# Moving ten label loads within one DMA queue: four to later places, six spread out

## What is computed

```python
e = stack([tbl_f[ids[:, f]] for f in range(50)], axis=1)      # 1024 x 50 x 300
q1 = attn_pool(e, mask, w1, b1, w2)                           # softmax-weighted sums of e
q2 = attn_pool(e, mask, w3, b3, w4)
h = concatenate([q1, q2], axis=1) @ w5 + b5                   # 1024 x 300
f6 = h @ w6 + b6
iu, ju = triu_indices(300, k=1)                               # 44850 pairs
g = (v @ v.T)[iu, ju]
cross = h[:, iu] * h[:, ju] * g
f7 = cross @ w7 + b7                                          # w7 is 44850 x 300
out8 = concatenate([f6, f7], axis=1) @ w8 + b8
z = einsum('bu,bku->bk', out8, label_embedding)               # labels: 1024 x 200 x 300
y = relu(relu(concatenate([z, dense_ctx], 1) @ W_top1 + b_top1) @ W_top2 + b_top2) @ W_top3
```

## Time and profile before

| | |
|---|---|
| time, median of 3 runs | 1852.51 us (1850.72 to 1853.8) |
| the profiled execution | 1854.63 us |
| its span | 1852.8 us |
| mean granted clock of PE | 0.963 |
| bytes moved by DMA | 561.70 MB, mean 303 GB/s |
| PE matmuls of L1000 | 5648, 1528.1 us busy |
| label loads | 200, 1200 KB each |
| w7 loads | 325, 320 of them of 750 KB |

### The profile page before, as it was taken

One profiled execution on the slowest core, in us unless ns is written; L12 is line 12 of the kernel. 1 busy time (PEld: TensorE's weight loads), 2 busy tenths in 40 slices (PEclk: granted clock), 3 DMA queues, 4 the chain that ended last, 5 costly groups with the idle time before them and its releaser, 6 DMA issues.

```text
span 1852.8 us, 26080 instructions
## 1 busy us (share of the span) xinstructions
PE 1690.2 (91%) x7084; PEld 1249.0 (67%) x7084; DVE 1666.4 (90%) x5850; ACT 1028.8 (56%) x3233; POOL 554.8 (30%) x413
## 2 busy tenths in 40 slices
PE   2788899999999999999999999999997999998751
PEld 1555567777777777777777777777775777775531
DVE  5998979989999889999999999999998888867676
ACT  3786684684466644466654664456653544454434
POOL 7777506827300135400077018500000000000053
PEclk8899999999999999999999999999998999998975
DMA  9488955757988688989768766997649999989975
GB/s 277 114 290 316 340 181 189 244 169 278 380 320 308 238 325 350 353 333 342 288 223 337 272 253 216 385 418 295 247 163 396 421 390 378 401 311 419 420 304 242
DMA packets 97054, 561.70 MB, mean 303 GB/s; under 512 B 15567, under 2 KB 15941, under 8 KB 71309
## 3 DMA queue, kind: packets, MB, share of 16 engines
q1 hardware_dynamic: 77629, 498.39, 69.7%
q0 software_dynamic: 19264, 61.64, 10.5%
q10 hardware_dynamic: 16, 0.00, 0.0%
HBM read 559.98 MB, written 0.00 MB: 302 GB/s over the span
## 4 chain that ended last, share of the span: by engine, by line
PE 54%; DVE 23%; DMA 10%; POOL 6%; issue 4%; ACT 2%; SPq 0%; DVEq 0%; ACTq 0%; POOLq 0%
PE acc L1000 47%; DVE junk L618 11%; DMA w_sb<-in_w 8%; DVE qa L660 6%; DVE prod L770 6%; POOL x L561 4%; PE coarse L849 2%; DMA lab<-in_labels 2%; POOL lab L561 2%; PE acc L915 1%; PE misc L922 1%; PE acc L896 1%; PE acc L899 1%; ACT waste L1120 1%; PE acc L881 1%
## 5 line engine op out<-in xcount | busy, mean ns | idle before, releaser
L1000 PE MATMUL acc<-w_sb,prod 128*128 128x300 f32 (+2 forms) x5648 | 1528.1, 421 | 58.8 <-DMA w_sb<-in_w 41.3
L1000 PEld LDWEIGHTS acc<-w_sb,prod 128*128 128x128 f32 (+2 forms) x5648 | 1043.2, 192 | 405.7 <-DMA w_sb<-in_w 51.8
L1225 ACT ACTIVATE prod<-prod,g_all 128x256 f32<-128x256 f32 (+4 forms) x1615 | 686.3, 470 | 465.9 <-DVE prod L770 463.5
L561 POOL DMA_INDIRECT x<-in_tbl,ids_sb x368 | 477.7, 1298 | 664.9 <-DVE qa L660 558.9
L770 DVE TENSOR_TENSOR prod<-fine,coarse 128x1280 f32<-128x1280 f32 (+4 forms) x325 | 423.3, 1308 | 102.9 <-PE coarse L849 100.9
L618 DVE SCALAR_TENSOR_TENSOR junk<-lab,heads 128x300 bf16<-128x300 f32 x1208 | 477.6, 461 | 12.7 <-DMA lab<-in_labels 12.2
L618 DVE SCALAR_TENSOR_TENSOR junk<-x,heads 128x300 bf16<-128x300 f32 x1128 | 445.2, 461 | 24.0 <-DMA x<-in_tbl,ids_sb 23.9
L660 DVE SCALAR_TENSOR_TENSOR qa<-x,ex,qa 128x300 f32<-128x300 f32 x612 | 275.6, 523 | 0.0
L592 POOL TENSOR_TENSOR x<-x,out 128x2400 f32<-128x2400 f32 x5 | 26.2, 5253 | 599.9 <-ACT out L1095 591.1
L1120 ACT ACTIVATE waste<-x 128x300 bf16<-128x300 f32 x368 | 161.8, 440 | 26.4 <-DMA x<-in_tbl,ids_sb 25.1
L1044 ACT ACTIVATE picked<-hh 128x256 f32<-128x256 f32 (+4 forms) x325 | 121.6, 375 | 0.0
(11 more groups left out here) (107 smaller groups left out, 518.9 us busy)
## 6 DMA issues: line engine op xcount, KB each, us to landing
w_sb<-in_w SPq DMA_DIRECT2D x320, 750.0 KB, 6.6
lab<-in_labels SPq DMA_DIRECT2D x146, 1200.0 KB, 8.6
x<-in_labels SPq DMA_DIRECT2D x54, 1200.0 KB, 9.8
x<-in_tbl,ids_sb POOLq DMA_INDIRECT x368, 5.4
w_sb<-in_w SPq DMA_DIRECT2D x5, 450.0 KB, 3.7
prod<-in_v_i SPq DMA_DIRECT2D x1, 710.0 KB, 4.7
prod<-in_v_j SPq DMA_DIRECT2D x1, 710.0 KB, 7.1
w_sb<-in_w SPq DMA_DIRECT2D x1, 703.1 KB
```

The costliest lines, as they stand in the source:

```text
L561: pool.indirect_dma_start(out=row_of(t, n), out_offset=None, in_=tables[n], in_offset=bass.IndirectOffsetOnAxis(ap=ids_sb[:, t, n:n + 1], ...
L1000: last = pe.matmul(acc[:, t % 3, 0:EMB], prod[0:rows, u % RING, m, t % 2 * P:(t % 2 + 1) * P], w7_sb[0:rows, u % W7_RING, m * EMB:(m + 1) ...
L1225: act.activation(chunk, chunk, ACT.Copy, scale=g_all[0:rows, pair:pair + 1]).then_inc(chunk_ready, 1)
```

## The change

Behind the planning, which stays as it is, the order of the list is edited. Slabs 0 to 3 are taken out and put back one each directly ahead of the w7 loads of units 58, 60, 62 and 64. Slabs 112 to 117 are taken out and put back from the place of slab 112 on, every second entry, so that what stood behind them moves up between them. The two stretches become w57 S0 w58 w59 S1 w60 w61 S2 w62 w63 S3 w64, and w246 S112 w247 S113 S110 S114 w248 S115 S111 S116 w249 S117 S118 S119 w250. Number, sizes, buffers, semaphores and waits of the loads are unchanged, and so are the programs of all other engines.

```diff
@@ -154,6 +154,7 @@
 COST = {"dots": 40, "wsums": 45, "slab": 32, "mask": 15, "normalise": 8, "pooled": 9}
 CROSS, UNIT, GATHER, LOAD_W7, LOAD_SLAB = (0, 8, 14), (0, 29, 57), 70, 20, 33
+FIRST_SLABS = 58
 FIRST_CROSS, GATHERED, FIRST_GATHER, PACE = 45, -230, 63, 75
@@ -259,8 +260,17 @@
         if kind == "pooled" and t == TILES - 1:
             switch = (nslab + 2 * SLOTS - 1) // SLOTS * SLOTS
-    loads.sort(key=lambda load: load[0])
-    return before, items, tail, pool_ticks, [load[1:] for load in loads], switch
+    loads = [load[1:] for load in sorted(loads, key=lambda load: load[0])]
+    early = [("slab", n) for n in range(SLOTS)]
+    loads = [load for load in loads if load not in early]
+    for n in range(SLOTS):
+        loads.insert(loads.index(("w7", FIRST_SLABS + 2 * n)), early[n])
+    spread = [("slab", n) for n in range(switch, switch + X_SLOTS)]
+    at = loads.index(spread[0])
+    loads = [load for load in loads if load not in spread]
+    for n, load in enumerate(spread):
+        loads.insert(at + 2 * n, load)
+    return before, items, tail, pool_ticks, loads, switch
```

## The result

The changed kernel takes 1841.1 us (median of five runs, 1839.9 to 1842.3) against 1851.2 of the kernel before, measured beside it (1850.0 to 1853.8). The ratio is 0.9938, with a 95% interval of 0.9928 to 0.9949; of 1851.2 us that is a gain of 11.5 us (9.4 to 13.3). The forecast was 1841.8 us and a gain of 10.7. The profiled execution has a span of 1839.3 us, 13.5 less than the 1852.8 of before.

What follows compares the result with a forecast made beforehand. PE (busy 91%) and DVE (90%) were taken to bound the kernel, with PE waiting for weight loads. 8.2 + 2.5 = 10.7 us brings the median 1852.5 to 1841.8 us; range 1837.5 to 1846.5.

Steps and rivals of the forecast that it cites:

- Term 1: Units 37 to 41: moving slabs 0 to 3 removes PE's 7.41 us wait before unit 37, worth 8.2 us.
- the lower bound: Units 37 to 41: the least Term 1 could give, 7.4 us, from DVE's and PE's own waits.
- DVE's part: Units 37 to 41: ACT moving by 8.2 asks 0.8 us more of DVE; if not covered, 7.4 stands.
- The new place: W7 loads 58 to 64: slabs 0 to 3 cost nothing there, covered by 11.9 us to spare.
- Rival 4: Units 54 to 63: labels fill the DMA engines where tile 3's gathers run; slower, 1861.4 us; chance 0.03.
- rival 5: Unit 37: the stall has another cause, gathers sharing the engines, so the edit fails; 1852.5 us; chance 0.05.
- Term 2: Units 247 to 253: spreading slabs 112 to 117 moves the 9.73 us wait down a full queue; worth 2.5 us.
- The line of 2.9 us per label load and 1.8 per weight load: From S112's landing at 1396.3, loads land one after another at 420 GB/s, perhaps 0.9 us later.
- a spell of low clock: Units 249 and 250: slow matmuls after a wait; free in unit 249, costing 2.0 us in unit 250.
- rival 1: Units 247 to 250: the queue is still late, so the second edit gives nothing; 1844.3 us; chance 0.13.

Runs made afterwards that it cites:

- e7: The changed kernel, but ACT's absolute sums of fields 5 to 24 of tile 2 read 30 of 300 columns: 1835.4 us, ratio 0.9918 to the kernel before.
- e1_first_only: The kernel before with only slabs 0 to 3 moved, slabs 112 to 117 together as before: 1843.1 us, ratio 0.9956 to the kernel before.
- e3: The changed kernel, but slabs 0 to 3 all directly ahead of w7 load 58: 1841.1 us, ratio 0.9951 to the kernel before.
- e8: The changed kernel, but slabs 0 to 3 two places apart from w7 load 38 on instead of 58: 1842.3 us, ratio 0.995 to the kernel before.
- e5_apart5: The changed kernel, but slabs 112 to 117 five places apart instead of two: 1854.9 us, ratio 1.0016 to the kernel before.
- e10_apart5_117: As e5_apart5, but slab 117 directly behind slab 116 instead of behind slab 126: 1847.0 us, ratio 0.9972 to the kernel before.
- e4_apart3: The changed kernel, but slabs 112 to 117 three places apart instead of two: 1841.0 us, ratio 0.9944 to the kernel before.
- e2_second_only: The kernel before with only slabs 112 to 117 spread two places apart, slabs 0 to 3 together as before: 1849.4 us, ratio 0.9988.

## Why the prediction was right

**Term 1** was forecast at 8.2 us and is 8.3 between units 34 and 41. Its steps hold one by one. PE has no wait for weights near 225 and its clock is 1.00 (220 to 228). ACT's copy starts at 227.70, right behind the unit's last scaling, which was to be the new limit, and e7 shows that ACT is that limit. It was taken from ACT's own row (8.21) and not from PE's or DVE's (7.41, 7.4), which is where the difference to the lower bound lies. DVE's part was left open; e7, in which only ACT's work is less and unit 41 comes sooner, shows that DVE did not hold anything back.

**The new place** was costed at nothing. The w7 loads from 58 to 64 whose landings are recorded have 7.9 to 11.6 us to spare (e1_first_only; the three of the changed kernel 10 or more), where over 8 was forecast: one, w64, is just under it. DMA moves 343 GB/s in 330 to 360, below the 388 worked out and below 420. Rival 4 had no ground, and e3 shows how much worse it can get before PE waits at all: four loads in a row, and still 0.3 us left. The price of 2.9 us for a label load was taken from a stretch without gathers; beside them it was 4.1 in the old stall. The spare time covered that. So rival 5 had something in it: the traces point to the gathers as what made the old stall longer, though they don't make it alone, as e8 shows at the same place. Its time of 1852.5 was also inconsistent, because the 2.5 us of term 2 would have stayed; it should have been 1850.

**Term 2** was forecast at 2.5 us and is 2.4. The line of 2.9 us per label load and 1.8 per weight load gave w249 at 1419.4 to 1420.3 in the time of before; in the changed kernel it landed at 1409.2, which is 1420.6 with the shift of 11.45 us added, so 0.3 us beyond the range. A wait of 2 to 3 us before unit 249 was forecast and is 2.05. The wait before unit 250 was to be 4.8 us by the sum (1426.0 to 1430.8), less what a spell of low clock in unit 249 takes of it. It is 2.82, and unit 249 took 7.7 us in place of 5.7. That unit 250 would pay a spell of low clock was part of the sum, and it did: four matmuls took 2.37 us where 1.25 is the rate elsewhere. Unit 250 starts 4.2 us earlier against unit 246, where 4.5 was forecast, and the spell takes 1.7 us back, where 2.0 was. The two misses of 0.3 us cancel, which is luck. Not foreseen was the 0.76 us for which unit 248 waits for ACT; it costs nothing, as unit 249 waits anyway.

**The rate of the queue** was the point on which rival 1 hung. It is 418 to 422 GB/s here in the three full stretches shown. The Trainium skill, page "DMA: Bandwidth & Descriptors", section Specifications, gives some 358 GB/s for a core as its share of HBM. In its section "Measured (HBM→SBUF, 128 partitions, SWDGE, issued from GpSimd)" the same page lists up to 425 GB/s for a single core with the other of its pair idle, and roughly 358 with both streaming. This kernel runs on one core, and the trace agrees with the higher figure, before the change (420) and after.

**What the sum left out** are 3 us that the profile shows and no edit explains (1.4 before unit 34 and 1.7 near unit 180). In the medians they don't show: 10.1 us lie between them, 11.5 by the ratio, and 10.7 were forecast. With differences of this size between single profiles, that the forecast time is met within 1 us says less for it than the two places do, each measured from a unit just ahead of it. The reason why equal stretches differ by 1 to 3 us from one profile to the next stays open.

## What to carry to other kernels

In this kernel's one queue, taken in order and with the DMA engines full, a load was late by the bytes that were issued ahead of it. Where that is so, spreading them out moves a wait, and removes only what other work can cover before the end of the line (here 2.4 of 9.7 us). A block of loads costs nothing where the next load is issued with more spare time than the block is long, so look for a place with slack; here either that or spacing was enough. Price the block in the stretch where it will stand: a label load took the line 2.9 us without gathers and 4.1 beside them. Before spreading further, write down when each spread load is wanted, and which load behind it needs a buffer that another of them frees.

## What the runs showed of the hardware

**The clock.** Waits of PE of about the same length do not have the same effect. After 2.05 and 2.82 us (changed kernel) four matmuls took 2.26 and 2.37 us; after 2.27 us (e5_apart5) and 2.58 us (e10_apart5_117) they took 1.28, full speed. In e4_apart3 1.96 us gave 1.58, in e2_second_only 2.12 gave 1.49 and 2.83 gave 1.74. In the stretches of the two new waits the granted clock is 0.79 and 0.81, between the two levels of 1.2 and 2.4 GHz, so some of that time was spent at the lower one. The length of a wait alone does not tell whether the clock falls; what else decides was not tried.

**The order of landing.** In the second place, where no gathers run, the loads landed as if the queue were one line of bytes: 18.8 us for w249, 20.8 us for S119, and half the bytes of six loads gave 8.7 us back. Where gathers took 21% of the DMA engines' time, the same line ran slower, 4.1 us per label load in place of 2.9. And a load that is ready does not pass one that stands ahead of it in SyncE's program: S117, with its buffer free, waited for S126's.
